# Seven score products instead of eight from the third pair of row tiles on, P's low halves moved to GpSimd, the mean's broadcast to ScalarE

## The reference, cut to what matters

```python
h = maximum(layernorm(x), 0)                  # x: 4096 x 256
lQ, lK, lV = masked_x @ Wlq, h @ Wlk, h @ Wlv + blv
gK, gV = mean(h, 0) @ Wgk, mean(h, 0) @ Wgv + bgv
s  = where(adj, lQ @ lK.T / 16, -1e9)         # 4096 x 4096
gs, es = (masked_x @ Wgq) @ gK.T / 16, masked_x @ Wes
m  = maximum(max(s, 1), maximum(gs, es))
le, ge, ee = exp(s - m), exp(gs - m), exp(es - m)
den = sum(le, 1) + ge + ee
res = le / den @ lV + ge / den * gV + ee / den * (masked_x @ Wev + bev)
out = x + maximum(res, masked_x)
```

## Time and profile before

| | us |
|---|---|
| median of 3 runs (733.49 to 735.16) | 733.9 |
| the profiled execution's own time | 733.93 |
| its span | 732.0 |
| TensorE busy | 721.8 |
| VectorE, ScalarE, GpSimd busy | 564.6, 531.5, 432.3 |

### The profile page before, as it was taken

One profiled execution on the slowest core, in us unless ns is written; L12 is line 12 of the kernel. 1 busy time (PEld: TensorE's weight loads), 2 busy tenths in 40 slices (PEclk: granted clock), 3 DMA queues, 4 the chain that ended last, 5 costly groups with the idle time before them and its releaser, 6 DMA issues.

```text
span 732.0 us, 15027 instructions
## 1 busy us (share of the span) xinstructions
PE 721.8 (99%) x5248; PEld 511.5 (70%) x5248; DVE 564.6 (77%) x1350; ACT 531.5 (73%) x706; POOL 432.3 (59%) x300
## 2 busy tenths in 40 slices
PE   8999999999999999999999999999999999999998
PEld 7666566666766767776767777676677777676777
DVE  6976788778787797778877787878878887876644
ACT  6873876777687777776877687777777777677690
POOL 4779589654555465556545655566546555654493
PEclk9999999999999999999999999999999999999999
DMA  9682587869778888987978797988879798878696
GB/s 301 132 178 61 123 164 157 168 142 211 154 173 172 169 161 152 206 152 175 170 167 162 153 204 132 204 150 179 176 166 165 154 205 146 181 161 183 118 184 151
DMA packets 364716, 121.93 MB, mean 167 GB/s; under 512 B 324832, under 2 KB 364640, under 8 KB 364640
## 3 DMA queue, kind: packets, MB, share of 16 engines
q1 hardware_dynamic: 364096, 120.44, 81.1%
q10 hardware_dynamic: 544, 0.52, 0.2%
HBM read 36.57 MB, written 4.19 MB: 56 GB/s over the span
## 4 chain that ended last, share of the span: by engine, by line
PE 84%; DVE 6%; issue 3%; ACT 3%; DMA 2%; POOL 1%; SPq 0%; DVEq 0%; ACTq 0%; POOLq 0%
PE ps_u L1114 14%; PE ps_u L1118 14%; PE ps_u L1116 14%; PE ps_x L1012 6%; PE ps_x L1013 6%; PE ps_x L1011 6%; PE ps_q L935 4%; PE ps_v L1011 3%; PE ps_v L1013 3%; PE ps_v L1012 3%; PE ps_w L1011 2%; PE ps_w L1012 2%; PE ps_w L1013 2%; DVE st L1329 1%; DMA hW<-bias 1%
## 5 line engine op out<-in xcount | busy, mean ns | idle before, releaser
L618 POOL TENSOR_TENSOR p_base<-s,p_base 128x1024 f16<-128x1024 f32 x112 | 242.3, 2164 | 227.1 <-ACT p_base L821 212.9
L1114 PE MATMUL ps_u<-v_rows,pT_base 128*128 128x256 f16 x968 | 263.8, 273 | 0.8 <-DMA pT_base<-bias 0.8
L1116 PE MATMUL ps_u<-v_rows,pT_base 128*128 128x256 f16 x968 | 263.8, 273 | 0.0
L1118 PE MATMUL ps_u<-v_rows,pT_base 128*128 128x256 f16 x968 | 263.8, 273 | 0.0
L784 ACT ACTIVATE bias<-adj,big 128x1024 f32<-128x1024 uint8 x127 | 156.5, 1237 | 130.6 <-DVE bmax L1482 126.4
L797 ACT ACTIVATE s<-s,negm,invc 128x1024 f32<-128x1024 f32 x128 | 157.0, 1227 | 9.5 <-DVE negm L1538 9.5
L821 ACT ACTIVATE p_base<-s 128x1024 f16<-128x1024 f32 x122 | 129.0, 1057 | 4.6 <-DMA pT_base<-p_base 0.8
L1114 PEld LDWEIGHTS ps_u<-v_rows,pT_base 128*128 128x128 f16 x968 | 94.7, 98 | 53.3 <-DMA pT_base<-bias 1.0
L1116 PEld LDWEIGHTS ps_u<-v_rows,pT_base 128*128 128x128 f16 x968 | 94.7, 98 | 52.2
L1482 DVE CUSTOM_DVE_ANT_0 s<-ps_x,bias 128x512 f32<-128x512 f32 x128 | 87.2, 686 | 48.8 <-PE ps_x L1013 45.3
L1118 PEld LDWEIGHTS ps_u<-v_rows,pT_base 128*128 128x128 f16 x968 | 94.7, 98 | 11.0
(11 more groups left out here) (242 smaller groups left out, 1265.8 us busy)
## 6 DMA issues: line engine op xcount, KB each, us to landing
adj<-adj SPq DMA_DIRECT2D x64, 256.0 KB, 3.2
pT_base<-p_base SPq DMA_TRANSPOSE x238, 3.2
s<-x SPq DMA_DIRECT2D x7, 512.0 KB, 7.9
f32q<-mx SPq DMA_DIRECT2D x14, 256.0 KB, 3.6
xm<-x SPq DMA_DIRECT2D x14, 256.0 KB, 3.0
xm<-mx SPq DMA_DIRECT2D x14, 256.0 KB, 3.5
out<-t_sb SPq DMA_DIRECT2D x14, 256.0 KB, 2.6
mxT_f<-mxT SPq DMA_DIRECT2D x4, 256.0 KB, 3.1
```

The source lines that it names most:

```text
L618: nc.gpsimd.tensor_tensor(p_rows(u)[:, 1], s32[:, p % NS, u % 2], p_rows(u)[:, 0], ALU.subtract).then_inc(s_plo, 1)
L1114: nc.tensor.matmul(acc, turn[:, 0, j], v_rows[:, kc, 0:D], start=opens, stop=False, skip_group_check=True)
L1116: nc.tensor.matmul(acc, turn[:, 0, j], v_rows[:, kc, D:2 * D], start=False, stop=False, skip_group_check=True)
L1118: done = nc.tensor.matmul(acc, turn[:, 1, j], v_rows[:, kc, 0:D], start=False, stop=end, skip_group_check=True)
```

## The change

`PC` becomes 8, so that periods 8 to 11 have seven products, and T3's sums, halves and q's sums come four periods earlier. `low_on_dve` holds for units 0 to 3 only; GpSimd makes the low halves of units 4 to 9 as well. On GpSimd all forms of group 1 come in period 4, T1 of group 2 ahead of q's sums in period 6 and T2 behind q's low half, the rest in periods 7 to 9. `keys_t3_high` waits for T1 of its group and for the last eight-product use of it. The mean's scaling and broadcast go to ScalarE (`mean_rows`, ahead of `v_high(12)`). SyncE loads adjacency tiles 5 and 6 ahead of the first transposition of P. On VectorE the scale of mx's rows comes ahead of the output passes in periods below `PC`, and two subtractions from the biases move behind `weights_low` in period 7.

```diff
--- before.py
+++ after.py
@@ -30,7 +30,8 @@
     DC = D // P
     NP = T // 2
     NPER = NP * NG
-    PC = 12
+    PC = 8
+    LOWS = 4
     QH = 3
     LAG_E = 5
     LAG_V = 6
@@ -253,7 +254,7 @@
             return PC <= p < NPER
 
         def low_on_dve(u):
-            return u // 2 + LAG_E < PC - 2
+            return u < LOWS
 
         V_AT = {2: (0, 1, 2, 3), 3: (4, 5), 4: (6, 7), 5: (8, 9), 6: (10, 11), 7: (12, 13)}
         HALVES = 3
@@ -474,12 +475,13 @@
                 sp.dma_start(dst[:, :], src.partition_broadcast(P)).then_inc(s_bc, 16)
             sp.dma_start(wev_sb[:, :, :], cols(Wev)).then_inc(s_wev, 16)
             load_mxT_q(2)
+            load_adj(5)
+            load_adj(6)
+            transpose_p(0)
 
             for p in range(4, NPER + LAG_E + 1):
-                if p + 1 < NPER:
+                if 7 <= p + 1 < NPER:
                     load_adj(p + 1)
-                if p == 4:
-                    transpose_p(0)
                 if p % NG == 0 and QH <= (p + 4) // NG < NP:
                     transpose_mx((p + 4) // NG)
                 if 1 <= p - LAG_E < NPER:
@@ -645,6 +647,8 @@
                 u = 2 * (p - LAG_E)
                 live = 0 <= u < 2 * NPER and not low_on_dve(u)
                 n = (p + 2) // NG
+                if p == 6:
+                    keys_t1(2)
                 if p % NG == 2 and 2 <= n < NP and NG * n >= PC:
                     q_sums(n)
                 if live:
@@ -655,16 +659,24 @@
                     finish(NP - 3)
                 if live:
                     p_low(u + 1)
+                if p == 6:
+                    keys_t2(2)
                 if p % NG == 3 and QH <= (p + 5) // NG < NP:
                     mx_low((p + 5) // NG)
                 n = (p - 12) // NG
                 if p % NG == 0 and 0 <= n < NP and n != NP - 3:
                     finish(n)
-                if p in (4, 6, 8):
-                    keys_t1(p // 2 - 1)
-                    keys_t2(p // 2 - 1)
-                if p in (5, 7, 9):
-                    keys_t4((p - 3) // 2)
+                if p == 4:
+                    keys_t1(1)
+                    keys_t2(1)
+                    keys_t4(1)
+                if p == 7:
+                    keys_t4(2)
+                    keys_t1(3)
+                if p == 8:
+                    keys_t2(3)
+                if p == 9:
+                    keys_t4(3)
             pool.wait_ge(s_xm_end, 32)
             nc.gpsimd.tensor_tensor(edge_rows[:, 1], edge_rows[:, 1], edge_rows[:, 0], ALU.add).then_inc(s_rest_end, 1)
             pool.wait_ge(s_e_end, 2)
@@ -822,9 +834,19 @@
 
             def keys_t3_high(g):
                 act.wait_ge(s_t3sum, g + 1)
+                act.wait_ge(s_t1, g + 1)
+                act.wait_ge(s_p7, PC - NG + g + 1)
                 nc.scalar.activation(plain(g, 0, 1, 0), ps_q[:, g % 2].rearrange("p (j q) -> p j q", q=P), ACT.Copy
                                      ).then_inc(s_t3hi, 1)
 
+
+            def mean_rows():
+
+                act.wait_ge(s_xbar, 1)
+                nc.scalar.activation(xbarT[:, :], ps_mean, ACT.Copy, scale=1.0 / (N * H_SCALE)).then_inc(s_gev, 1)
+                act.wait_ge(s_gev, 1)
+                for c in range(DC):
+                    nc.scalar.activation(xbar_bc[:, c], ones32[:, :], ACT.Copy, scale=xbarT[:, c:c + 1]).then_inc(s_gev, 1)
 
             act.dma_start(wk_t, WlkT.rearrange("(c p) d -> p c d", p=P)).then_inc(s_wqk, 16)
             act.dma_start(xg[:, 0, 2:4], x_groups[0][:, 2:4]).then_inc(s_x[0], 16)
@@ -885,6 +907,7 @@
             v_high(10)
             v_high(11)
             mask_bias(7)
+            mean_rows()
             v_high(12)
             v_high(13)
             mask_bias(8)
@@ -1123,17 +1146,15 @@
             def keys_t3_sum(g):
 
                 if g < 2:
-                    pe.wait_ge(s_qf, PC - 3)
+                    pe.wait_ge(s_qf, 7)
                 else:
-                    pe.wait_ge(s_c2, 2)
+                    pe.wait_ge(s_t3, 2)
                 for k, (c, hl) in enumerate(((1, 0), (1, 1), (0, 0), (0, 1))):
                     last = nc.tensor.matmul(ps_q[:, g % 2, :], eye16[:, 1 - c], plain(g, c, 1, hl), start=k == 0,
                                             stop=k == 3)
                 last.then_inc(s_t3sum, 1)
 
             def es_values(n):
-                if n == 0:
-                    pe.wait_ge(s_t3, 2)
                 if n < QH:
                     pe.wait_ge(s_mxf, 16 * (n + 1))
                 if n == QH:
@@ -1708,11 +1729,6 @@
             out_pair(5)
             v_low(10)
             v_low(11)
-            dve.wait_ge(s_xbar, 1)
-            nc.vector.tensor_scalar(xbarT[:, :], ps_mean, 1.0 / (N * H_SCALE), None, ALU.mult).then_inc(s_gev, 1)
-            dve.wait_ge(s_gev, 1)
-            for c in range(DC):
-                nc.vector.tensor_scalar(xbar_bc[:, c], ones32[:, :], xbarT[:, c:c + 1], None, ALU.mult).then_inc(s_gev, 1)
             out_pair(6)
             v_low(12)
             dve.wait_ge(s_wg, 32)
@@ -1738,10 +1754,6 @@
                     dve.wait_ge(s_sidec, 2)
                     side_top(0)
                     side_top(1)
-                if p == 7:
-                    dve.wait_ge(s_gev, 5)
-                    nc.vector.tensor_tensor(gv_b[:, :], gv_b[:, :], blv_b[:, :], ALU.subtract).then_inc(s_gev, 1)
-                    nc.vector.tensor_tensor(bev_b[:, :], bev_b[:, :], blv_b[:, :], ALU.subtract).then_inc(s_gev, 1)
                 u = 2 * (p - LAG_E)
                 low = 0 <= u < 2 * NPER and low_on_dve(u)
                 old = p - 1
@@ -1753,12 +1765,12 @@
                         row_max(0)
                     if low and u:
                         p_low(u)
+                    if step == 3:
+                        mx_scale((p + 5) // NG)
                     out11(p)
                     out12(p)
                     if p == 4:
                         p_low(0)
-                    if step == 3:
-                        mx_scale((p + 5) // NG)
                     if project:
                         q_rows(m)
                     if low:
@@ -1770,27 +1782,18 @@
                         keys_t3_low(1)
                     if project:
                         q_row_scales(m)
-                    if p == 8:
-                        row_max(1)
                     if p == 5:
                         weight_tops()
                     if p == 6:
                         weight_scales()
                     if p == 7:
                         weights_low()
-                    if p == 9:
-                        wev_low()
-                    if step == 1 and p >= 9:
-                        weights((p - 9) // NG)
-                    if step == 2 and p >= 10:
-                        side_rows((p - 10) // NG, 0)
-                        side_rows((p - 10) // NG, 1)
-                    if step == 3 and p >= 11:
-                        es_rows((p - 11) // NG)
-                        local_rows((p - 11) // NG)
+                        dve.wait_ge(s_gev, 5)
+                        nc.vector.tensor_tensor(gv_b[:, :], gv_b[:, :], blv_b[:, :], ALU.subtract).then_inc(s_gev, 1)
+                        nc.vector.tensor_tensor(bev_b[:, :], bev_b[:, :], blv_b[:, :], ALU.subtract).then_inc(s_gev, 1)
                 else:
                     done = (p - 9) // NG
-                    ended = done < NP - 1
+                    ended = 0 <= done < NP - 1
                     if wino(old):
                         out12(old)
                     if p < NPER:
@@ -1829,6 +1832,8 @@
                         side_rows(done, 1)
                     if step == 0 and p < NPER:
                         row_max(n)
+                    if p == 9:
+                        wev_low()
                     if step == 1 and ended:
                         weights(done)
                     if step == 3 and ended:
```

## The result

The kernel after takes 741.8 us (median of 4 runs, 741.52 to 742.12) against 733.9 us for the one before: a ratio of 1.0104, interval 1.0091 to 1.0116, so it is 1% slower. The profiled execution took 741.97 us, its span is 740.2 us. The forecast was 737.0 us: the side was right, the size was not, and 741.8 lies just above the range of 731.5 to 741.

What follows compares the result with a forecast made beforehand. TensorE, busy 99% of the span, was taken as the bound: 733.93 - 5.3 of gains + 4.4 + 2.2 + 1.8 of new holes = 737.0 us. Range 731.5 to 741; the forecast's own 735.4 to 739, also written 735.4 to 739.5.

Steps and rivals of the forecast that it cites:

- ScalarE's wait for q's sums: Ahead of q_high, near 87: ScalarE idle some 3 to 4.5 us until GpSimd has made the sums.
- the hole behind unit 3: TensorE's wait in period 7 behind unit 3's low half: not named in the prediction, so given no cost.
- The mean's hole: TensorE's 1.67 us wait at 56.08 for the mean's broadcast on VectorE: claimed to go whole, bounds 1.2 and 1.67.
- the 1.05 us: TensorE's wait at 89.04, start of period 7, for period 6's output pass: claimed to close through the earlier tile load.
- The twelve matmuls: Periods 8 to 11 on TensorE, seven products each: 12 matmuls at 0.216 us fewer, a gain of 2.6 us.
- First hole: Start of period 8: TensorE there at 98.5, p1 able to start at 102.9 after unit 5's low half; cost 4.4 us.
- Second hole: Projection behind period 8, waiting for T3 of group 3 after GpSimd's T1: cost 2.2 us, between 0.8 and 3.5.
- Third hole: Periods 9 to 11, output waiting for GpSimd's low half of unit 10: cost 1.8 us, between 0 and 4.
- Rival (c): Period 8 begins at half clock behind the first hole: 5 us more, 2.2 covered, 739.8 us; chance 0.12.
- Rival (a): GpSimd has room, so the first and second holes go: 728.6 to 731 us; chance 0.16.

Runs made afterwards that it cites:

- experiment 1: Kernel before with the mean's broadcast on ScalarE and adjacency tiles 5 and 6 loaded earlier: 731.3 us; with the broadcast alone: 731.8 us.
- the last kernel of 7: Kernel after with sums first, units 4 and 5 on VectorE, T4 of group 3 later, VectorE operations moved, fewer key-sum additions (part of computation omitted): 729.2 us.
- the first of 1: Kernel before with the mean's broadcast on ScalarE and adjacency tiles 5 and 6 loaded ahead of the first transposition of P: 731.3 us.
- experiment 5: Kernel after with matmuls nobody reads filling TensorE's two long holes, clock full throughout: 742.8 us with long fillers, 741.45 us with short ones.
- the better order: Kernel after with q's sums first, low halves of units 4 and 5 on VectorE, T4 of group 3 later, four VectorE moves: 733.4 us.
- experiment 7: Key sums of groups 2 and 3 cut to one addition each, omitting computation: 736.4 us on the kernel after, 729.2 us on a reordered one.
- experiment 2: Kernel after with q's sums ahead of T1 of group 2: 739.3 us; low halves of units 4 and 5 on VectorE: 741.0; both: 737.0.
- LOWS = 6: Kernel after with the low halves of units 4 and 5 back on VectorE, GpSimd's order unchanged: 741.0 us.
- the sums first: Kernel after with q's sums and q's low half ahead of T1 of group 2 on GpSimd: 739.3 us.
- both moves: Kernel after with q's sums and low half ahead of T1 of group 2, and units 4 and 5's low halves on VectorE: 737.0 us.

## Why the prediction was wrong in size

The step that failed is the pricing of the waits: ScalarE's wait for q's sums was sized 3 to 4.5 us and measured 6.85, the hole behind unit 3 was put at nothing and measured 2.05, the third was sized 1.8 and measured 4.1, and the fall of the clock was left to a rival. By term:

- **Gains, right in sum.** The mean's hole went whole, and experiment 1 gives both small edits together what I gave them (2.7). Their split was wrong: most of the 1.05 us closed with the mean's rows and not with the early loads. The twelve matmuls (2.6) show in the traces of the last kernel of 7 and the first of 1: the former is 1.7 us ahead in period 13, with 0.8 of hole before it.
- **"ScalarE ... could start q_high near 83 to 84.5, but q_high now waits for the sums".** The root is the right one, but the wait was 6.85 us where I had 3 to 4.5, for two reasons. ScalarE was there at 82.1, and "GpSimd ends the forms of group 1 at 79.0; its work up to there doesn't move" failed: two of its operations took 1.67 and 2.09 us where their like take 0.61 and 1.16, so it ended at 80.25 (in the kernel before one took 2.02), and two subtractions of T1 took 3.49 instead of 2.40.
- **The hole that I left out, 2.05 us.** I wrote that "the exponentials of unit 3 and all later ones stand behind it" and then followed only unit 5. Unit 3's low half is on VectorE, ahead of period 6's last two output passes: the same kind of wait, half a period on, as the 1.05 us that I had just closed. A wait has to be followed through every consumer behind it, the nearest first.
- **First hole, 4.4 forecast, 4.3 measured**, but both ends were 1.7 us later than mine (104.56 against 102.9, 100.24 against 98.5), since the hole of period 7 had moved TensorE as far as the sums had moved the low half. The link was sized right, the agreement to 0.1 is luck.
- **Second hole, 2.2 forecast, none.** The mechanism is real; it didn't show because TensorE came late, by 1.7 us from the holes before and by 1.5 from the slow clock. With the clock kept full it is 1.35 us, in the better order 2.47.
- **Third hole, 1.8 forecast, 4.1 measured** (0.64 + 0.58 + 2.90). The mechanism was the one named (the low half of unit 10, a wait near's 2.63: it was 2.75), but I left out what stands on VectorE between that and out12, 3.6 us of side rows.
- **Rival (c) happened**, and twice, but smaller than I had it: behind the first hole 3.2 us were slow and cost 1.5, where I had 5 us more and 2.2 of it covered, and a second stretch that I hadn't named cost as much again. That its 739.8 is near has luck in it. By the sum, 5.0 us too low is 2.05 - 0.1 - 2.2 + 2.3 + 3.1 = 5.2. But experiment 5 shows that the clock is hardly a cause of its own: with it full the time is the same within the noise (0.4 us lower). What was mis-sized is how late GpSimd and the order behind it are.
- **The range.** The forecast's own is written as 735.4 to 739 and as 735.4 to 739.5; the bounds of its holes (0.8 to 3.5 and 0 to 4) give 733.8 to 740.5. The measured time lies above each of them.
- **Rival (a)**, that GpSimd had room, is refuted by p1's wait of 4.16 us, and experiment 7 shows what its work costs; its condition ("If the chain to unit 5's low half were 4 us shorter than I make it, the first hole goes and with it the second") is too simple: with ScalarE's wait gone in experiment 2, new holes of 1 to 2 us came where TensorE arrived earlier.

## What to carry to other kernels

When a saving on the full engine asks for its operands earlier, add up the work of the preparing engine over the stretch, not only its next step: here it was busy 80.6 of 90 us and no order of the queues tried gave more than break-even. Nor is that sum enough, as 73.8 of 90 us in the wrong order still left 5.1 us of waits. When a new wait is put ahead of a shared queue, walk every instruction behind it to its consumer, beginning with the nearest. And take small edits out of a large change and time them alone: two small edits of this one were worth 2.7 us, the rest cost 10.5.

## What I had not expected of the hardware

- The clock's fall behind a hole is not settled by the hole's length. In the kernel after it fell behind a wait of 2.74 us that ended at 143.91: it was full until about 145.2, 1.3 us into the work behind the wait. In the kernel with LOWS = 6 the same wait, 2.72 us at 143.90, left it full, and so did those of 2.72 and 2.73 us in the kernels with the sums first and with both moves. All six waits from 3.56 to 4.16 us in these runs had a fall. The windows of the kernel with LOWS = 6, the first around its hole of 4 us and two behind the other:

```profile
103.00:107.00 4.00, 2.67 (x10) 1.46 (x11) 4.00 (x7) 3.97 (x6) 3.86 (x4) 0.66 1.05 219
143.00:146.00 3.00, 2.10 (x15) 1.41 (x16) 2.74 (x7) 2.06 (x2) 0.00 (x0) 1.00 1.03 220
146.00:149.00 3.00, 3.00 (x18) 2.30 (x17) 0.69 (x1) 2.94 (x6) 1.43 (x1) 1.00 0.97 217
```

  I have no explanation for the difference, and no run was made for it.
- VectorE's smallest operations can stretch beside GpSimd: one scaling of 128x2 elements took 1.96 us while GpSimd made a low half, the next one, in GpSimd's pause, 0.17, so 0.2 us on paper can be 2 on the path. In the kernel after, from 45 us on, 8 of the 16 float32 scalings of this size that ran mostly beside a GpSimd instruction took over 0.5 us, and none of the other 87 over 0.23. Why 8 did and 8 did not is open.

```profile
98.05 1.96 DVE L1479 TENSOR_SCALAR mcl<-mmax 128x2 f32<-128x2 f32 x1
100.05 0.17 DVE L1481 TENSOR_SCALAR mscale<-mcl 128x2 int32<-128x2 int32 x1
```

```profile
97.86 2.13 POOL L620 TENSOR_TENSOR p_base<-s,p_base 128x1024 f16<-128x1024 f32 x1 [0.72 <-ACT p_base L833]
```
